# Moving one batch's output projection two slots later in a post-norm attention and mixture-of-depths kernel, with the gather, one norm's roots and the last weight splits

## The reference

```
scores = einsum('bhki,bhqi->bhkq', k, q) / sqrt(HEAD); causal mask; softmax
out    = combined @ W_out + b_out
x      = layernorm(x + out)
scores = einsum('bsd,d->bs', x, w_router); top_idx = top_k(scores, S/2)
h      = gelu(selected @ W1 + b1); processed = h @ W2 + b2
x      = layernorm(x.at[idx].add(sigmoid(score) * processed))
```

## Time and profile before

| | |
|---|---|
| time, median of 3 | 2497.37 us (2494.77 to 2498.66) |
| the profiled execution's own time | 2497.64 us |
| its span, first to last instruction | 2495.8 us |
| TensorE matmul busy | 2437.9 us, 98% of the span |
| VectorE, ScalarE, GpSimd busy | 1677.7, 1227.0, 1566.2 us |
| mean granted TensorE clock | 0.993 |
| chain that ended last, by engine | PE 83%, POOL 11%, DVE 2%, issue 1%, ACT 1% |

### The profile page before, as it was taken

The page is one execution under the profiler, slowest core; times in us unless marked ns, Lnnn a source line. Parts: engine busy times, 40 slices in busy tenths (PEclk is TensorE's granted clock), DMA queues, the critical chain, the costliest instruction groups (busy, mean ns, idle before and its releaser), DMA issues.

```text
span 2495.8 us, 40908 instructions
## 1 busy us (share of the span) xinstructions
PE 2437.9 (98%) x14104; PEld 1798.0 (72%) x14104; DVE 1677.7 (67%) x4384; ACT 1227.0 (49%) x2211; POOL 1566.2 (63%) x1481
## 2 busy tenths in 40 slices
PE   8999999999999999999999999998999999999997
PEld 6666676777677767676767667763788888888886
DVE  6767778778777777777888787775755544553533
ACT  3665566666566666666666666666531111111110
POOL 2877888788877888877888888885323132221311
PEclk9999999999999999999999999998999999999999
DMA  4233445335344444534434354343421011010100
GB/s 178 95 128 117 161 138 199 129 124 187 136 146 162 145 145 141 175 133 166 157 129 161 125 180 145 128 162 97 169 64 43 19 34 33 26 34 26 32 20 17
DMA packets 167649, 287.72 MB, mean 115 GB/s; under 512 B 23258, under 2 KB 58138, under 8 KB 166172
## 3 DMA queue, kind: packets, MB, share of 16 engines
q1 hardware_dynamic: 160276, 268.26, 31.1%
q0 software_dynamic: 7168, 16.85, 2.1%
HBM read 117.23 MB, written 65.11 MB: 73 GB/s over the span
## 4 chain that ended last, share of the span: by engine, by line
PE 83%; POOL 11%; DVE 2%; issue 1%; ACT 1%; DMA 0%; SPq 0%; POOLq 0%; DVEq 0%; ACTq 0%
PE PS L1623 14%; PE PS L1602 14%; PE PS L1464 11%; POOL Pa L902 10%; PE PS L1549 10%; PE PS L1515 9%; PE PS L1567 9%; PE PS L1472 8%; PE PS L1477 6%; PE PS L1484 2%; POOL Pm L858 1%; PE PS L1439 1%; PE PS L1583 0%; DVE nm L1130 0%; DVE xTl L1223 0%
## 5 line engine op out<-in xcount | busy, mean ns | idle before, releaser
L902 POOL TENSOR_TENSOR Pa<-Pa,Pm 128x512 f32<-128x512 f32 (+1 forms) x602 | 751.9, 1271 | 129.3 <-ACT Pm L1012 106.7
L1549 PE MATMUL PS<-Qp,Kp 128*128 128x512 f32 (+3 forms) x1536 | 491.0, 355 | 8.7 <-ACT Pm L1012 4.1
L1515 PE MATMUL PS<-Kp,Qp 128*128 128x512 f32 (+3 forms) x1536 | 485.3, 351 | 6.6 <-DVE nm L1130 5.5
L1012 ACT ACTIVATE Pm<-PS 128x512 f32<-128x512 f32 (+1 forms) x643 | 358.3, 568 | 243.7 <-PE PS L1549 194.0
L1130 DVE TENSOR_REDUCE nm<-PS 128x1 f32<-128x512 f32 x512 | 344.7, 687 | 157.2 <-PE PS L1515 156.9
L902 POOL TENSOR_TENSOR Pa<-Pa,P 128x512 f32<-128x512 f32 (+1 forms) x297 | 371.9, 1274 | 64.7 <-ACT P L1012 53.6
L1515 PEld LDWEIGHTS PS<-Kp,Qp 128*128 128x128 f32 x1536 | 276.2, 189 | 105.4 <-issue 41.6
L974 ACT ACTIVATE G<-PS,b1c 128x512 f32<-128x512 f32 x128 | 88.2, 689 | 536.5 <-PE PS L1602 520.3
L1549 PEld LDWEIGHTS PS<-Qp,Kp 128*128 128x128 f32 x1536 | 274.8, 189 | 93.5 <-ACT Pa L1012 29.0
L1138 DVE CUSTOM_DVE_ANT_0 PS<-PS,maskA 128x384 f32<-128x384 f32 (+3 forms) x512 | 246.3, 509 | 121.9 <-PE PS L1515 119.9
L1623 PE MATMUL PS<-W2h,Gs 128*128 128x512 f32 x1024 | 316.6, 390 | 1.1 <-DVE W2l L1228 1.1
(11 more groups left out here) (154 smaller groups left out, 4261.2 us busy)
## 6 DMA issues: line engine op xcount, KB each, us to landing
Qp<-nat SPq DMA_DIRECT2D x192, 256.0 KB, 2.5
Kp<-nat SPq DMA_DIRECT2D x192, 256.0 KB, 2.9
o_s<-Of SPq DMA_DIRECT2D x64, 256.0 KB, 2.1
xb<-in_x SPq DMA_DIRECT2D x64, 256.0 KB, 3.4
Ot<-o_s SPq DMA_DIRECT2D x64, 256.0 KB, 3.0
h_s<-hs SPq DMA_DIRECT2D x64, 256.0 KB, 2.1
out<-xb SPq DMA_DIRECT2D x64, 256.0 KB, 2.2
x_raw<-in_xt SPq DMA_DIRECT2D x15, 1024.0 KB, 6.4
```

Of the source, the lines that this page charges most:

```text
L902: e.tensor_tensor(to, to, probs(u, k)[:, h0:h0 + many, 0:w], ALU.add).then_inc(s["padd"], many)
L1012: e.activation(probs(u, k)[:, hh[0]:hh[-1] + 1, 0:w], tile_bank(j)[:, 0:len(hh) * w].rearrange("p (h n) -> p h n", n=w), ACT.Exp).then_inc ...
L1515: ins = e.matmul(to, Qp[:, u % 4, h_, qt * P:qt * P + P], Kp[:, (2 * i + k0 // 512) % 4, h_, 0:w], start=True, stop=True)
L1549: ins = e.matmul(tile_bank(j)[:, x_ * w:x_ * w + w], Kp[:, (2 * i + k // 4) % 4, h_, k % 4 * P:k % 4 * P + P], Qp[:, u % 4, h_, 512 - w:51 ...
```

## The change

Four things are altered, and no arithmetic of the reference.

1. Batch 6's `O` tiles 48 to 55 (8b + t) go to slots 60, 61, 62, 63, 63, 64, 64, 65 in place of 58 to 65. Slots 58 and 59 have none, slots 63 and 64 have two each. `earliest` places the second ones at 63:8 and 64:4.
2. The gather of batch 0 goes from 64:2 to 64:5, the load of its list from 64:0 to 64:3.
3. `NORM_FIRST` goes from 62:0 to 65:6. The roots of tiles 4 to 7 of batch 6 are then ScalarE's; POOL keeps those of batch 7.
4. W1's last four half splits go from 64:14, 65:0, 65:2, 65:4 to 64:9, 64:11, 64:13, 64:15.

```
-LAG = 2
-GATHER = 63 * 16 + 18
-NORM_FIRST = 62 * 16
+LATE_SLOT = 8 * (B - 1) + 2
+LATE_TILES = ((), (), (48,), (49,), (50,), (51, 52), (53, 54), (55,))
+LAG = 2
+GATHER = 64 * 16 + 5
+NORM_FIRST = 65 * 16 + 6
...
-    o = slot - 10
-    out = [("O", o // 8, o % 8)] if 0 <= o < 8 * (B - 1) else []
+    first = LATE_SLOT - 10
+    tiles = LATE_TILES[slot - LATE_SLOT] if LATE_SLOT <= slot <= U + 1 else (slot - 10,)
+    out = [("O", o // 8, o % 8) for o in tiles if 0 <= o < (8 * (B - 1) if slot >= LATE_SLOT else first)]
...
+    if job[0] == "O" and job[1] == B - 2:
+        return {4: 8, 6: 4}.get(job[2], 0)
...
-        w1_at = [BEATS * (U - 1) + x_ for x_ in (14, 16, 18, 20, 30, 32, 34, 36)]
+        w1_at = [BEATS * (U - 1) + x_ for x_ in (14, 16, 18, 20, 25, 27, 29, 31)]
```

## The result

The changed kernel takes 2506.89 us (median of 9 runs, 2503.27 to 2509.72), the kernel before 2497.11 us in the runs beside it. The ratio is 1.0036, 95% interval 1.0028 to 1.0045: slower by some 9.8 us. My forecast was 2497.5 us, no change, with 2490 to 2503.5 as its range. It was wrong, and the range doesn't hold the time. The profiled execution of after is the slowest of the nine, 2509.72 us with a span of 2508.0. In all that follows it has to be kept apart from the median. Lines of the changed kernel's code stand 5 higher than before (L1567 is L1572, and so on).

The account below looks back on a forecast made before the run. TensorE was taken to bound the kernel, except POOL in slot 63, with ScalarE bounding late slot 64 after the change. Terms: -1.9 - 3.6 - 0.5 + 4.6 + 1.7 + 0 = +0.3; forecast 2497.5 us, no change, range 2490 to 2503.5.

Parts of the forecast that it names:

- A: Slots 58 and 59 lose their output tiles: the pair takes 51.06 us, 1.9 us gained (0 to 5.4).
- B: Slot 63 up to the sum of unit 61: roots leave POOL, which bounds it; 3.6 us gained (2.0 to 4.3).
- C: From the sum of unit 61 to slot 64's first output tile: 4.9 us instead of 5.37, 0.5 us gained.
- the charge for the split: In slot 63, 0.7 us lost to VectorE's split of one more Os inside POOL's stretch.
- D: Slot 64, first output tile to products at 1728.73: new TensorE stop, more ScalarE work; costs 4.6 us (3 to 5.5).
- E: Products of unit 63: the clock may fall behind the nine thin tiles; 1.7 us lost.
- the middle I took: For the clock at unit 63's products: 1.7 us lost, between 0 and 3.4.
- F: W1's last splits and the last tile's roots: the turn waiting 1.89 us comes no earlier; 0 (up to 1.1 gained).
- the one for slower: Half clock lasts from unit 63's nine thin tiles on, through later blocks and tiles: 2505 us, chance 0.17.

Follow-up runs that it names:

- e1: Changed kernel with POOL's bias addition for tile 4 of batch 6 four beats into slot 63 instead of eight; 2502.23 us, 1.0023.
- b1: Kernel before with only the roots of tiles 4 to 7 of batch 6 moved to ScalarE; 2494.97 us, 0.9996.
- e4: Changed kernel with the gather of batch 0 and the load of its list at their places of before; 2505.10 us, 1.0033.
- d4: Changed kernel with the gather on POOL made to wait until ScalarE has copied the product of unit 62 (Of); 2503.75 us, 1.0028.
- e3: Changed kernel with W1's last four half splits at their places of before; 2504.70 us, 1.0028.
- d2: Kernel before with every part of the change but the tiles: roots on ScalarE, later gather, W1's last splits sooner; 2494.36 us, 0.9991.
- b2: Kernel before with only the gather of batch 0 three beats later; 2494.46 us, 0.9994.
- d1: Kernel before with the roots of tiles 4 to 7 of batch 6 on ScalarE and the later gather; 2491.14 us, 0.9978.
- b4: Kernel before with the move of the tiles alone; gather, roots and W1 splits as before; 2505.85 us, 1.0039.
- e2: Changed kernel with the roots of tiles 4 to 7 of batch 6 on POOL again; 2509.38 us, 1.0046.

## Why the prediction was wrong

By the table the changed kernel's trace differs from the one before by -0.1 in the pair, +2.4 in "63", +5.6 in "64", +1.7 in "turn" and +1.5 in "up": 11.1 of the 12.1 us between the two profiled executions. The forecast had -1.9, -3.6, +4.1, +1.7 and 0. The largest miss is slot 63, with 6.0 us.

*A, slots 58 and 59: right.* Eight traces have both tiles out of the pair. In seven it takes 51.13 or 51.14 us; I had 51.06, a gain of 1.9. In the profiled execution of after, TensorE fell to half clock behind the small waits that the missing tiles leave (the sum of unit 57 took 1.88 us), and the pair took 52.82. That is a matter of one execution and explains part of why it is slower than the median.

*B, slot 63: the step that failed.* "TensorE gets 2.7 us for one more tile, and has 55.60 - 49.55 = 6.05 us of gaps [...], so the tile fits." It fits on TensorE. For slot 63 I costed the tile's matmuls and one Os split. Its bias addition I had only in C, as 1.27 us ahead of a mask, and I never asked what waits for its result: the residual, the statistics, the roots, and behind them the last row maxima and an exponential of unit 62. By the order of the Table the addition came behind all of POOL's work for unit 61, and everything after it was late by that. POOL's own part of B was right: its stretch, from 1669.07 to 1700.65, is 2.4 us shorter than before (33.97), where the roots less the charge for the split came to 2.8. But "what leaves POOL counts in full" no longer held once another path ended last. I had 3.6 us gained and the trace shows 2.4 lost. Of these 6.0 us e1 gives 3.9 back; b1 against e1 shows the other 2.2, which a second tile costs there even when well placed: POOL's stretch is 1.6 us longer with the 1.29 us addition inside it (32.62 and 31.06), and the sum comes 0.71 us after its end, where b1 has 0.05. The charge of 0.7 for two engines in each other's way is seen as 0.46 in after, beside the second tile's Os split on VectorE (0.95 us, where another took 0.69):

```profile
1688.32 0.95 DVE L1334 TENSOR_TENSOR Os<-Ot,Os 128x512 fp32r<-128x512 f32 x1
```

```profile
1688.68 1.09 POOL L863 TENSOR_SCALAR_AFFINE_SELECT Pm<-Pm 128x512 f32<-128x512 f32 x1
...
1696.39 0.63 POOL L863 TENSOR_SCALAR_AFFINE_SELECT Pm<-Pm 128x512 f32<-128x512 f32 x1
```

A mask at 1694.37 took 1.09 us too, beside VectorE's router score. In e1 POOL's addition at 1698.22 took 1.72 us, where the one at 1688.82 took 1.29, and it overlaps VectorE's Os split (1697.31 to 1698.81, 1.50 us where another took 0.69). By the rule of the Trainium skill in SBUF — State Buffer, section "Who interferes with whom", the one that comes second would wait for the end of the one that has the shared port; the trace agrees in direction, for both engines.

*C: the number right, by luck.* 4.81 us, I had 4.9. I had it as two bias additions and a mask on POOL and then TensorE at full clock. In after the additions were over at 1703.09, ahead of the sum, and the mask at 1706.22; no product waits for them. The 4.81 us are TensorE's own blocks from 1706.30, without a gap and most of them at half clock (the first and the third took 1.94 and 1.89 us).

*D, slot 64: right in its mechanism, too small by 1.5.* I had 4.6, the trace has 6.1. The stop for the second tile's low part is 2.23 us (I had 2.2). From Of to the end of the last P3 exponential ScalarE has no gap, 11.3 us (I had 11.8, before 7.83). Missing is the late copy Of, 1.7 us. e4 and d4 show that it comes with the place of the gather: the first moves it ahead, the second behind, and in both Of follows its product at once.

*E: right in its mechanism, but that the middle I took was met is luck.* 1.7 us lost: products and sums at 1737.40 and 1739.11 took 1.94 and 1.91 us, the other two ran at full clock. In the eight traces with all tiles moved "turn" is 1.4 to 2.4 us longer than before. *F: right in the sum.* The turn still waits 1.89 us. But W1's splits sooner weren't worth 0 for the kernel: they are the 2.0 us within D, and e3 and d2 measured 2.2 and 3.2.

*Not foreseen:* in after TensorE fell to half clock once more behind the turn, 1.5 us in "up". e1 and e4 don't have it (24.3 us), b1, b2 and d1 do (25.6, 25.8 and 25.8), so it doesn't belong to the tiles.

Of the rivals, the one for slower had its time nearly right (2505) and its cause wrong. I gave it a half clock that lasts from the thin tiles of unit 63 on. There it held for 3.4 us of products and sums. What the forecast lacked was above all the wait behind the bias addition in slot 63; the stop for the second low part in slot 64 it had. What gave me no warning was that in slot 63 I worked a tile's cost out from its 12 matmuls and one split, and never listed its other instructions on POOL and VectorE in their order against unit 62's exponentials and the row maxima.

The parts, each by its own runs: tiles alone +9.8 us (b4), roots on ScalarE -1.1 alone and -2.5 with the tiles (b1, e2), the later gather -1.6 alone and +1.8 with the tiles (b2, e4), W1's splits sooner +2.2 to +3.2 (e3, d2). By time alone only the tiles' part and d2's 3.2 against d1 are clear of the spread; for the others the traces named above speak. The gather shows why parts aren't to be priced on the kernel before alone: with a second tile in slot 64 the wait it removes is already covered, and it runs just when Of falls due.

## What to carry to other kernels

When a job is moved into a slot that seems to have room, list every instruction it has on every engine, in the order in which each will stand there, and ask what is queued behind each; room on the engine of its matmuls says nothing about the others. Where one small instruction of the moved job stands at the end of a busy engine's block, and other engines' critical work stands in program order behind what needs its result, its place is worth more than its duration (1.3 us long, 3.9 to 4.7 us of time here). Look for all such paths: with the one over ScalarE gone, the one over VectorE held TensorE for 4.53 us (e2). Try the parts of a change alone: here two of the four make a kernel that is faster than both (2491.14 us, 0.9978), and the other two are what costs.

## What the runs showed of the hardware

The copy Of on ScalarE started 1.28 to 2.22 us after the start of its last product, in place of 0.46 to 0.48, in four of the fourteen traces: after, e1, e2 and e3. In these four that product ended between the end of POOL's second indirect DMA and the end of the fourth, and in after VectorE's residual addition was late at the same moment (1725.44, its last matmul done by 1724.7). In the ten others the gathers were over, hadn't begun or were at the first or second, and Of started at once. Moving the gather either way removes the delay (e4, d4). In three of the four (after, e1, e3) Of starts 0.62 or 0.63 us after the end of the fourth DMA; in e2 it starts during the third. By the code Of also waits for the store out of its buffer, that of unit 60, issued at 1680.79 in after; VectorE's addition, late with it, has no such wait, so the store isn't the cause. What passes between the two isn't settled: no run tells whether it is a semaphore's update, the DMA traffic or the instruction supply.

TensorE's granted clock fell to 0.50 behind stretches in which it had waited (in after, 0.50 from 1735 on, behind 5 us with 1.72 of matmuls), and which stretches it hit differed between executions of nearly the same kernel: the pair of slots 58 and 59 in one of eight traces, "up" in after and not in e1. So single traces of this kernel differ by 1 to 3 us for this alone, and the differences between the experiments are to be read beside the waits of their traces.
